# Grouped-query attention: each round of sixteen 32x32 matmuls waits for the first tile of the round before

## The reference

```python
q = hidden_state @ Wq + bq
k = encoder_hidden_state @ Wk + bk
v = encoder_hidden_state @ Wv + bv
scores = jnp.einsum('bkgld,bksd->bkgls', q, k) * scale
scores = scores + encoder_attention_mask[:, :, None, :, :]
attn = jax.nn.softmax(scores, axis=-1)
out = jnp.einsum('bkgls,bksd->bkgld', attn, v)
...
x = out @ Wo + bo + hidden_state
# and a layer norm of x with gamma and beta
```

## Time and profile before

| | before |
|---|---|
| runs | 1750.47, 1751.70, 1752.71 us |
| median | 1751.7 us |
| profiled execution, first to last instruction | 1749.3 us |
| median of the runs over that span | 2.4 us |
| TensorE busy | 1602.6 us (92%) |
| VectorE busy | 1448.7 us (83%) |
| ScalarE busy | 1385.7 us (79%) |
| GpSimd busy | 935.7 us (53%) |
| mean granted clock of TensorE | 0.974 |

### The profile page before, as it was taken

One profiled execution on the slowest core, in us unless ns is written; L12 is line 12 of the kernel. 1 busy time (PEld: TensorE's weight loads), 2 busy tenths in 40 slices (PEclk: granted clock), 3 DMA queues, 4 the chain that ended last, 5 costly groups with the idle time before them and its releaser, 6 DMA issues. The chain is left out here.

```text
span 1749.3 us, 38438 instructions
## 1 busy us (share of the span) xinstructions
PE 1602.6 (92%) x14048; PEld 1110.0 (63%) x14048; DVE 1448.7 (83%) x2773; ACT 1385.7 (79%) x3186; POOL 935.7 (53%) x731
## 2 busy tenths in 40 slices
PE   3898879999899989999899998999989999999986
PEld 2665556576566765676576775667666676667654
DVE  4489878789788996889888898789988899788886
ACT  3578868769888787978889789787888878887794
POOL 5426433526754458534675448662585545856382
PEclk8999999999999999999999999999999999999998
DMA  9669987646885578664796567965678646875331
GB/s 178 186 148 227 241 232 199 182 135 168 250 257 144 138 187 286 188 154 122 209 288 185 130 175 192 287 178 127 174 238 252 158 133 170 292 208 150 84 114 67
DMA packets 357292, 325.02 MB, mean 186 GB/s; under 512 B 145776, under 2 KB 248176, under 8 KB 357104
## 3 DMA queue, kind: packets, MB, share of 16 engines
q1 hardware_dynamic: 357104, 322.56, 67.5%
HBM read 244.85 MB, written 83.89 MB: 188 GB/s over the span
## 5 line engine op out<-in xcount | busy, mean ns | idle before, releaser
L1941 PE MATMUL bank<-ring_hi,w_sb 128*128 128x512 f32 x2368 | 785.5, 399 | 32.1 <-issue 19.2
L1725 ACT ACTIVATE probs<-probs,shift 128x512 f32<-128x512 f32 x1024 | 726.9, 713 | 92.1 <-DVE shift L1826 91.0
L1839 DVE STREAM_TRANSPOSE turned_p<-probs 128x2048 f32<-128x2048 f32 x256 | 585.7, 2297 | 154.3 <-PE bank L2021 149.3
L1826 DVE CUSTOM_DVE_ANT_0 probs<-bank,mask_l 128x512 f32<-128x512 f32 x1024 | 643.1, 680 | 56.3 <-PE bank L2001 37.2
L1626 POOL TENSOR_TENSOR w_sb<-w_raw,w_sb 128x512 fp32r<-128x512 f32 x320 | 412.1, 1297 | 413.8 <-ACT w_sb L1682 413.7
L1941 PEld LDWEIGHTS bank<-ring_hi,w_sb 128*128 128x128 f32 x2368 | 444.4, 189 | 149.9 <-issue 42.6
L1941 PE MATMUL bank<-ring_lo,w_sb 128*128 128x512 f32 x1184 | 467.9, 395 | 0.0
L2001 PE MATMUL bank<-k_stack,q_stack 96*128 96x512 f32 x1024 | 358.9, 414 | 12.7 <-DVE shift L1826 10.0
L2021 PE MATMUL bank<-turned_p,v_all 32*32 32x512 f32 x8192 | 307.9, 642 | 65.8 <-DVE turned_p L1839 48.6
L1638 POOL TENSOR_TENSOR ring_lo<-x_t,ring_hi 128x512 fp32r<-128x512 f32 x168 | 214.7, 1291 | 144.9 <-ACT ring_hi L1694 144.4
L2001 PEld LDWEIGHTS bank<-k_stack,q_stack 96*128 96x128 f32 x1024 | 186.1, 189 | 143.3 <-issue 62.9
(11 more groups left out here) (75 smaller groups left out, 933.2 us busy)
## 6 DMA issues: line engine op xcount, KB each, us to landing
w_raw<-w_d SPq DMA_DIRECT2D x144, 256.0 KB, 3.7
q_stack<-q_hi_d SPq DMA_DIRECT2D x128, 256.0 KB, 4.3
w_raw<-in_L_xattn_Wo_dram SPq DMA_DIRECT2D x128, 256.0 KB, 3.0
q_hi_d<-part_hi SPq DMA_DIRECT2D x64, 256.0 KB, 3.9
q_lo_d<-part SPq DMA_DIRECT2D x64, 256.0 KB, 5.0
q_stack<-q_lo_d SPq DMA_DIRECT2D x64, 256.0 KB, 3.9
v_all<-v_d SPq DMA_DIRECT2D x256, 64.0 KB, 2.2
out_dram<-y_sb SPq DMA_DIRECT2D x32, 512.0 KB, 3.0
```

The lines of the kernel that those rows point to most:

```text
L1725: nc.scalar.activation(probs[:, st % 2, h, :], probs[:, st % 2, h, :], ACT.Exp, scale=-1.0, bias=shift[:, g % 2, i:i + 1], accum_out=sums[ ...
L1826: nc.vector.tensor_tensor_reduce(out=probs[:, st % 2, h, :], in0=S_ps[h][:, :], in1=mask_l[:, st, :], scale=-1.0, scalar=HIGHEST, op0=ALU. ...
L1839: nc.vector.transpose(turned_p[:, :, :, st, :].rearrange("p j h c -> p h j c"), probs[:, st % 2, :, :].rearrange("p h (j c) -> p h j c", c ...
L1941: mm = nc.tensor.matmul(C[c][:, :], w_sb[:, n_w, (1, 0, 0)[third], d % 4, :], (hi, lo, hi)[third], start=(n == 0), stop=(n == 23))
```

## The change

A new semaphore `pv_round` is incremented by the first matmul of a round, tile (0, 0), in the first three rounds of each product. Each of rounds two to four begins with a wait for the increment of the round before. Three increments a group make the expected value 3 G + jj.

```diff
-        pv_done, pv_out = sem("pv_done"), sem("pv_out")
+        pv_round, pv_done, pv_out = sem("pv_round"), sem("pv_done"), sem("pv_out")
...
                     for jj in range(4 * n // PV_PARTS, 4 * (n + 1) // PV_PARTS):
+                        if jj > 0:
+
+                            pe.wait_ge(pv_round, 3 * G + jj)
                         for c in range(4):
                             for r in range(4):
                                 j = 4 * jj + c
...
                                                       start=(jj == 0), stop=(jj == 3))
+                                if c == 0 and r == 0 and jj < 3:
+                                    mm.then_inc(pv_round, 1)
                     if n == PV_PARTS - 1:
                         mm.then_inc(pv_done, 1)
```

## The result

| | before | after |
|---|---|---|
| runs | 1749.74 to 1753.69 us (5) | 1757.80 to 1761.87 us (5) |
| median | 1751.7 us | 1758.87 us |
| ratio | | 1.005, 95% interval 1.0037 to 1.0062 |
| profiled execution, first to last instruction | 1749.3 us | 1755.6 us |
| that execution's own time | not listed | 1757.8 us |

The change makes the kernel slower by 7.2 us between the medians; the interval of the ratio is 6.5 to 10.9 us. The span of the profiled execution grew by 6.3 us. The forecast was +1.8 us, within what cannot be told from no change. The median lies just inside the upper end of the range given, 1759 us.

What follows compares the result with a forecast made beforehand. TensorE, fullest at 92%, was taken as the bound, with products on the path of both full engines. 64 products at +0.03 us gave 1.9 us: span 1751.2, plus 2.4 for runs, forecast 1753.5 us; range 1744.5 to 1759 us.

Steps and rivals of the forecast that it cites:

- Who stands behind a burst: Each product of 64 matmuls with values: TensorE and VectorE both wait on it, so added time reaches the end nearly fully.
- Increments and waits as instructions, cost 0: Three increments and three waits in each product were claimed to cost 0 as instructions.
- second slower rival: In each product, an increment or wait costs its own step, 0.03 us each; 5.8 us more, 1759.4 us; chance 0.08.
- What the wait holds: At each later round's start, the first load waits for the previous round's first-tile second pass and its increment; start at 1.08.
- return time: From the first tile's second pass ending to the waiting load's start: taken as 0.06 us, bounds 0.04 and 0.12.
- lead tile: In round two before the change, one tile starts at +0.86 us, ahead of the other fifteen from +1.05; the wait removes this.
- 0.43 + 0.59 + 0.06 = 1.08: Round period with the wait: way to second pass, that pass, increment's return; replaces 1.06, giving +0.03 us a product.
- faster rival: In later rounds, the queue fills behind the wait, tiles start 0.007 us apart; 4.5 us less, 1747.2 us; chance 0.25.
- first slower rival: At the waits, the increment takes longer to return; at 0.09 us, 5.8 us more, 1757.5 us; chance 0.19.
- signs of being wrong: 0.007 us steps throughout after pauses, return over 0.07 us, or a product's time not reaching the end because half-clock stretches shift.

Runs made afterwards that it cites:

- one wait in round two: Kernel after the change with its three increments a product but only the wait in front of round two; ratio 1.0022 to the kernel before.
- fourth tile: Kernel after the change with the increment moved from the first to the fourth tile of a round, waits kept; ratio 1.0132 to the kernel before.
- 63 increments: Kernel after the change without waits, every matmul of a product but the last incrementing `pv_round`; ratio 1.0161 to the kernel before.
- last tile: Kernel after the change with the increment moved from the first to the sixteenth tile of a round, waits kept; ratio 1.030 to the kernel before.
- increments only: Kernel after the change with its three increments a product and all waits left out; ratio 1.0007 to the kernel before.
- waits long met: Kernel after the change with two waits a product, each for an increment of two rounds before; ratio 1.0004 to the kernel before.
- inner loops exchanged: Kernel before the change, no semaphore or wait, with `for r` outside `for c` in the product; ratio 1.0014 to the kernel before.

## Why the prediction was wrong

**Who stands behind a burst: right, but "nearly one for one" was too little.** All of a longer burst reaches the end, and more with it. Over the runs, 64 times the excess of a burst and the excess of the ratio are: one wait in round two 3.1 and 3.9 us; the change 5.6 and 8.8 us (6.5 to 10.9); fourth tile 13.2 and 23 us; 63 increments 23.5 and 28 us; last tile 46.9 and 53 us. The surplus is taken up below, under the granted clock.

**Increments and waits as instructions, cost 0: right within 0.005 a burst** (increments only, waits long met). The second slower rival is ruled out for three increments, but its price, 0.03 each, turned out real once all matmuls carry one.

**What the wait holds: the mechanism was right.** The lead tile is lost, the first tile's chain becomes the period, the return time is short: the first release was forecast at 1.08 and came at 1.07.

**The step that failed: "the first tile now starts a round only 0.43 + 0.59 + 0.06 = 1.08 after it started the last one".** The period measured is 1.10. The return time is not at fault: 1.07 less the 1.02 at which the second pass ends leaves 0.05 to 0.06. The term that was mis-sized is 0.43, the way from the first pass to the second. In the second round of the kernel after, in windows of 1 ns at +1.50 and +1.53 of the product at 794.26 (passes in flight in the first bracket):

```profile
795.76:795.77 0.00, 0.00 (x16) 0.00 (x0) 1.00 0.00 0
795.79:795.79 0.00, 0.00 (x17) 0.00 (x0) 1.00 0.00 0
```

The seventeenth pass, the first tile's second one, is not yet there 0.43 after the release at 1.07, and is there at 0.46. I had read 0.43 off a tile whose first load went 0.03 before its pass (loads from 791.74, passes from 791.77). Behind a semaphore wait the load and the pass are released together. The trace of before had that case already, in a product that was released by a transpose, the one at 734.67. Loads of it:

```profile
734.67 0.25 PEld L2021 LDWEIGHTS bank<-turned_p,v_all 32*32 32x32 f32 x32 [2.04 <-DVE turned_p L1839]
735.13 0.10 PEld L2021 LDWEIGHTS bank<-turned_p,v_all 32*32 32x32 f32 x1 [0.21 <-issue]
```

There the load of the next round goes at 735.13, 0.46 after the start, and in the product at 791.77 it goes at 0.43. Nine of the 50 products at full clock throughout are of this kind, and last 4.464 in place of 4.455. The rows were there and I chose among them without asking which case the new wait makes. My own sum even had 0.45 between the two passes of the last tile; in the starts of the trace all fifteen tiles behind the first have 0.449 to 0.455 there, in the first round of the product at 791.77. That the 0.025 is the time of a weight load that nothing covers (a load is recorded as 0.10) is argued and not shown.

The sum with the measured terms: 1.308 + 2 x 1.098 + 0.451 + 0.587 = 4.542, as measured; the forecast had 1.30 + 2 x 1.076 + 0.45 + 0.59 = 4.49, which is 0.037 over 4.455 and which I then rounded down to +0.03. The excess measured is 0.087. Of the missing 0.057, 2 x 0.022 = 0.044 is the period, 0.008 is the start of the last tile of round two, which moves from 1.30 to 1.31 already with the increments alone, and the rest is rounding. In time that is 5.6 us in place of 1.9 us.

**The faster rival: its premise was half right.** Instructions do collect behind a semaphore wait and then start 0.007 apart, if everything older has left (wait for the last tile). It gains nothing, since completions are 0.017 to 0.018 apart even where starts are 0.007 apart. This is also what the 0.017 of rounds two to four is: the next round's loads come in as the tiles before them complete, and with an increment on every tile both distances grow to 0.0425 together.

**The first slower rival** (a loss of twice what the period exceeds 1.06) had the right form, with another cause for the excess.

**A second term, put at nothing: the granted clock.** The prediction took none of it into its sum and named it among its signs of being wrong. In the traces the granted clock is full or half at any moment. Its mean over the profiled execution is 0.974 before and 0.971 after; 93 us were at half the clock before, 105 us after. By stretches, the batch of the earlier trace rows that had 0.99 reads after the change:

```profile
1086.40:1293.80 207.40, 197.84 (x1758) 130.29 (x1756) 178.54 (x344) 172.18 (x396) 116.61 (x91) 0.98 0.70 194
```

The runs show it too. The five of the kernel after have 0.969 to 0.972; the 67 runs of the kernel before that the experiments were timed against have 0.975 in the median. Within these 67 a run with a mean clock lower by 0.001 takes 0.83 us longer (a fitted line, correlation -0.68; the fastest run is 1747.8 us at 0.977, the slowest 1758.2 us at 0.970). The last column of this table is an estimate: the excess after that line has taken all runs to the same clock. For the three kernels at 0.965 to 0.967 the line is drawn beyond the clocks that it was fitted to.

| kernel | 64 x excess of a burst, us | excess of the ratio, us | mean clock of the runs | excess at the same clock, us |
|---|---|---|---|---|
| one wait, round two | 3.1 | 3.9 | 0.974 | 3.1 |
| after | 5.6 | 8.8 | 0.971 | 5.3 |
| wait for the fourth tile | 13.2 | 23 | 0.967 | 16.6 |
| 63 increments | 23.5 | 28 | 0.965 | 20.5 |
| wait for the last tile | 46.9 | 53 | 0.966 | 46.0 |
| inner loops exchanged | 0 | 2.5 | 0.973 | 0.7 |

So the surplus of the change, about 3 us over the 5.6, is of the size that its lower clock goes with.

**What stays open.** Why the clock is lower is not shown. It is lower in every kernel here with bursts of 4.54 and more, but a little in the one with exchanged loops too, whose bursts are not. What the estimate leaves, up to 3.4 us either way, is open as well. In the profiles line 2021 or 2024 as a whole grew by 17.7 us where the median burst accounts for 13.2 (fourth tile), and by 30.3 us where it accounts for 23.5 (63 increments): bursts that fall in stretches at half the clock are longer, and of their time 59 and 63 us were at half the clock, against 48 us before. After the change itself it was 43 us, and its line grew by only 3.8 us.

## What to carry to other kernels

A wait for one's own earlier tile turns throughput into latency. Its price here was the tile's whole way (first pass, second pass, completion, return; 1.098) less the period that the queue gave already (1.058), once for each round that has no lead to spend, and moving the wait by one instruction made it free. Compare the granted clock of the runs before putting all of a difference down to the change. When a duration is to be used behind a new wait, take it from rows where that instruction was itself released by a wait. A pause that lets a queue fill is worth something only if starts, and not completions, set the pace.

## What was not expected of the hardware

- Sixteen 32x32 tiles whose second passes start 0.007 us apart complete about 0.017 us apart (release at +1.07, +1.14 and +1.34 us for a wait on tile 1, 4 and 16). The ends of matmuls in the records, start plus 0.587 us, are modelled and don't show it.
- With an increment on every matmul, each adds 0.026 us to that distance (0.0425 us in place of 0.017); with one tile in sixteen incrementing, a product is only 0.005 us longer.
- The second pass of the first tile of a product follows its first by 0.429 us if the load of the first went 0.03 us ahead of it, and by 0.453 us if load and pass were released together.
- A weight load that waits for an increment of its own engine starts 0.042 us after that increment arrives (median of the 192 waits of the kernel after).
